# A fused attention and expert kernel: the last two batches get a program of their own

## The chip, the cores and the metric

One NeuronCore of a Trainium2 chip. The metric is the device time of the kernel in microseconds (us); a comparison takes the median of several runs.

## The reference

32 batches of 256 tokens with 128 features. Attention with 16 heads of 8 features, with a cubic "stablemax" in place of softmax, then four experts of which each token uses the best two by a router:

```python
x = x + attn_ref(layernorm(x), w_qkv, w_out, b_out)
x = x + ffn_ref(layernorm(x), router_w, router_b, w1, w3, w2)
# ffn_ref, for T tokens, E = 4 experts, F = 512, K = 2:
probs = softmax(xf @ router_w + router_b)
top_p, top_i = top_k(probs, K);  top_p = top_p / sum(top_p)
gates = zeros((T, E)).at[arange(T)[:, None], top_i].add(top_p)
h = silu(einsum('td,edf->etf', xf, w1)) * einsum('td,edf->etf', xf, w3)
expert_out = einsum('etf,efd->etd', h, w2)
out = einsum('te,etd->td', gates, expert_out)
```

All is float32.

## The kernel before

Every engine has a program written out by hand (blocks `sync`, `gpsimd`, `scalar`, `vector`, `tensor`), and the engines meet at semaphores. Each program is a chain of slots n = -2 to 33, a `first_half` and a `second_half` each; `over_batches` unrolls the first six and the last six and loops over those between. A slot works on several batches at once: in slot n the scores and weights of batch n are in hand, batch n-1 has its attention output, residual sum, second normalization and router, and batch n-2 has its experts. So slots 32 and 33 hold little but the experts: in slot 32 those of batch 30 and the attention output of batch 31, in slot 33 the experts of batch 31 alone.

TensorE. `weighted_values(i, off, g)` (L926) multiplies group g of the weights with the values, g = 0, 1, 2 in the second half of slot n and g = 3 early in the next slot. The output is transposed (L1022), normalized by VectorE, transposed again (L1033), multiplied by the output projection (L1043). The residual sum is normalized and transposed (L1105), and the router product is L1121. The up projections of a batch are eight units u = 0 to 7, each an a half (`up_a_unit`, w1) and a b half (`up_b_unit`, w3) of six matmuls (L908; each operand is split in a high and a low part and three of the four products are taken). Unit 0 runs at the end of a slot's second half, units 1 to 7 in the next first half. All a halves go to one bank `up_a`; b halves to `up_b`, with units 3, 5 and 7 in a third bank. The down projection `down(c, e)` (L1090) sums the four experts in one accumulation per block c of 128 tokens, in `up_b`; so the gate has to be in the hidden values before it. A matmul of float32 operands shows as two records.

ScalarE. SiLU of an a half (L554), the copies of the attention output (L581, L594), the logarithm and exp of the four groups of weights (L608, L613, the weights are exp(-log(...))), and ln and exp of the small inverse square roots (L623, L626) and of the router (L640). SiLU and exp/log need different tables, loaded at L538 and L604.

VectorE. `hidden(u)` (L677) multiplies the SiLU with the b half into `hid`; `normalized` (L696, L701), `attention_added` (L713), `statistics` (L752, L755), the router's steps ending in `gates` (L837 to L847), and `experts_added` (L786), which adds the down projection of both blocks to `y_acc`.

GpSimd. `gate_hidden` (L422) multiplies a unit of `hid`, where tokens run along the free axis, with `gate_all`, the gates copied to all partitions. It also does the inverse square root's Newton steps (L460 to L479), the scaling by it (L484), the split of the normalized sum (L497, L500) and the ranks of the router (L505 to L517).

SyncE issues the DMAs, among them the gates to `gate_scratch` in memory (L394), `gate_all` from it (L342) and the store of `y_acc` (L389).

Of the kernel before, what the change touches and what calls it, by code (L numbers as in the profile page):

```python
# [5 lines left out]
def attention_then_experts_kernel(nc: bass.Bass, x: bass.AP, w_qkv: bass.AP, w_out: bass.AP, b_out: bass.AP,  # L6
# [32 lines left out]
    C = S // 128  # L39
    G = H // 4  # L40
    FB = F // 128
    NB = E * FB
    U = G * C
# [6 lines left out]
    UP = NB // 2  # L50
# [8 lines left out]
    with ctx:  # L59
# [24 lines left out]
        q_tile = sb("q_tile", [128, G, S], F32R)  # L84
# [54 lines left out]
        spare = banks[:, 1:3, :].rearrange("p a t -> p (a t)")  # L139
        router_out = up_b[:, C * D:C * D + C * E].rearrange("p (c e) -> p c e", c=C)  # L140
        misc = ctx.enter_context(nc.psum_tensor("misc", [128, 512], F32))
        b_bank = [banks[:, 2, :] if u in (3, 5, 7) else up_b for u in range(UP)]
        score_buf = [(sc[:, 0, :], sc[:, 1, :], spare)[u % 3] for u in range(U)]

# [75 lines left out]
        gated = sem("gated")  # L220
        down_full = sem("down_full")
        acc_ok = sem("acc_ok")
        stored = [sem(f"stored{i}") for i in range(2)]

        TILED = 16 * 2 * TERMS
# [8 lines left out]
        def has(i, off):  # L234
            return not isinstance(i, int) or 0 <= no(i, off) < B
# [10 lines left out]
        def over_batches(eng, half_a, half_b):  # L246

            for n in range(-2, 4):  # L250
                half_a(n // 2, n % 2)
                half_b(n // 2, n % 2)
            with eng.Fori(2, B // 2 - 2) as i:
                for off in range(2):
                    half_a(i, off)
                    half_b(i, off)
            for n in range(B - 4, B + 2):
                half_a(n // 2, n % 2)
                half_b(n // 2, n % 2)


        def blank_stacks(eng, par):
# [27 lines left out]
        def _(sp):  # L290
# [82 lines left out]
            def second_half(i, off):  # L373
                n = no(i, off)
                m_split_at = value(n + 2)
                added, out_at = value(n - 1), address((n - 2) * S * D)
                gates_at, gates_read = value(GATE * n), value(16 * (n - 1))
                xn_used, x_from = value(n + 3), address((n + 3) * S * D)
                if has(i, off + 3):
                    sp.wait_ge(xn_ok, xn_used)  # L380
                    sp.dma_start(x_in[:], batch_at(x, x_from)).then_inc(x_loaded, 16)
                if has(i, off + 1):
                    par = (off + 1) % 2
                    sp.wait_ge(m_ok, m_split_at)
# [5 lines left out]
                if has(i, off - 1):  # L390
# [3 lines left out]
                    sp.dma_start(gate_scratch, gates[par][:].rearrange("p c e -> p (c e)")).then_inc(gates_out, 16)  # L394

            over_batches(sp, first_half, second_half)
            for par in range(2):
                sp.wait_ge(stored[par], 16 * (B // 2))

# [2 lines left out]
        def _(pool):  # L402
# [49 lines left out]
            def second_half(i, off):  # L452
# [69 lines left out]
                if has(i, off):  # L522
# [4 lines left out]
                        last = nc.gpsimd.tensor_tensor(x_resb[:, c, :], x_res[:, c, :], b_out_all[:], ALU.add)  # L527
                    last.then_inc(xres_ok, 1)

            over_batches(pool, first_half, second_half)  # L530


        @block.scalar
        def _(act):
# [66 lines left out]
            def second_half(i, off):  # L601
# [31 lines left out]
                for g in range(G):  # L633
# [7 lines left out]
                    if has(i, off):  # L641
                        weights_of(g)

            act.wait_ge(consts_v, 1)
            over_batches(act, first_half, second_half)


        @block.vector
        def _(dve):
# [81 lines left out]
            def second_half(i, off):  # L731
# [156 lines left out]
                if has(i, off + 3):  # L888
                    input_statistics(n + 3)

            dve.wait_ge(consts_ok, 4)
            over_batches(dve, first_half, second_half)


        @block.tensor
        def _(pe):
# [35 lines left out]
            def up(u, dst, hi, lo, full):  # L932

                for half in range(2):
                    e, f = divmod(2 * u + half, FB)
                    fs = slice(f * 128, (f + 1) * 128)
                    last = exact(dst[:, half * S:(half + 1) * S], (hi[:, e, fs], lo[:, e, fs]),
                                 (xn2_hi[:], xn2_lo[:]))
                last.then_inc(full, 1)

            def up_a_unit(i, off, u):
# [6 lines left out]
            def up_b_unit(i, off, u):  # L948
                m = no(i, off)
                if u < 3:  # L950
                    after(pe, hid_ok, UP * m + u)
                elif u == 3:
                    pe.wait_ge(o_ok, min(m + 2, B) if isinstance(i, int) else m + 2)
                else:
                    pe.wait_ge(hid_ok, UP * m + u - 1)
                if u == 0:
                    after(pe, acc_ok, m)
                    pe.wait_ge(lg_ok, m + 1)
                up(u, b_bank[u], w3_hi, w3_lo, b_full)

            def distances(i, off, u):

# [89 lines left out]
            def second_half(i, off):  # L1052
# [80 lines left out]
                def queries_and_keys():  # L1133
                    m = n + 2
                    pe.wait_ge(xnT_ok, m + 1)
                    if has(i, off + 1):
                        pe.wait_ge(m_ok, n + 2)
                    nc.tensor.matmul(misc[:, 0:S], proj_T[:, 0, :], xn_T[:], start=True, stop=True)
                    nc.tensor.matmul(misc[:, S:2 * S], proj_T[:, 1, :], xn_T[:], start=True,
                                     stop=True).then_inc(qk_full, 1)  # L1140
# [30 lines left out]
                    up_b_unit(i, off - 1, 0)  # L1171
                if has(i, off + 2):
                    queries_and_keys()
                if has(i, off) and not (isinstance(i, int) and n == 0):
                    weighted_values(i, off, 2)

            over_batches(pe, first_half, second_half)


# [25 lines left out]
```

## Time and profile before

| | |
|---|---|
| median of three runs | 1187.17 us (1183.64 to 1187.72) |
| the profiled execution | 1186.13 us, span 1184.4 us |
| TensorE busy | 1108.0 us (94%), 10116 matmul records |
| VectorE busy | 970.1 us (82%) |
| ScalarE busy | 1007.1 us (85%) |
| GpSimd busy | 736.9 us (62%) |
| costliest group | L422 on GpSimd, 256 times, 405.4 us, 1624 ns each |

The span runs from the first to the last instruction of one profiled execution. Busy times of TensorE are modelled at the end of each record, and records overlap. A chain row is a piece of the work that ended last, followed backwards from the last instruction. "PE" is TensorE, "DVE" VectorE, "ACT" ScalarE, "POOL" GpSimd, "SPq" the DMA issues of SyncE.

### The profile page before, as it was taken

The page shows a single profiled execution, that of the slowest core. Times are in us where ns is not written, and L with a number is a line of the kernel's source. Part 1 is how long each engine was busy: PE and PEld are TensorE (multiplying, and loading weights), DVE is VectorE, ACT ScalarE, POOL GpSimd, SP SyncE. Part 2 cuts the span into 40 slices and gives each one's busy share as a digit, 9 for nine tenths or more (in the row PEclk, how much of TensorE's full clock was granted, in tenths as well). Part 3 has the DMA queues.
Part 4 walks back from the last instruction along what each step waited for, and adds up shares of the span by engine and source line. Part 5 has one row for each costly group of instructions (what it writes and reads, how often), then busy time and mean ns, then how long its engine had stood idle before and what let it go on. Part 6 is the DMA issues. An engine that isn't in the chain of part 4 may idle for free.

```text
span 1184.4 us, 29551 instructions
## 1 busy us (share of the span) xinstructions
PE 1108.0 (94%) x10116; PEld 945.0 (80%) x10116; DVE 970.1 (82%) x1804; ACT 1007.1 (85%) x1033; POOL 736.9 (62%) x961
## 2 busy tenths in 40 slices
PE   2468999999999999999999999999999999999987
PEld 1346888888888888888888888888888888888876
DVE  4577898988888898888889888889898888989632
ACT  0578999888999998899999888999988889998852
POOL 5415576766656767665676766667676666666564
PEclk9997999999999999999999999999999999999999
DMA  4523223333322333333223333322333332233000
GB/s 122 195 82 105 90 86 111 118 116 116 104 89 89 95 115 116 121 105 92 90 85 115 119 118 110 97 90 80 116 116 116 115 101 89 89 98 112 29 24 28
DMA packets 129779, 118.57 MB, mean 100 GB/s; under 512 B 15880, under 2 KB 124104, under 8 KB 129736
## 3 DMA queue, kind: packets, MB, share of 16 engines
q1 hardware_dynamic: 128584, 116.97, 31.8%
q10 hardware_dynamic: 1152, 1.05, 0.3%
q8 instruction: 25, 0.41, 0.1%
q14 instruction: 18, 0.15, 0.0%
HBM read 95.75 MB, written 21.10 MB: 99 GB/s over the span
## 4 chain that ended last, share of the span: by engine, by line
POOL 32%; PE 27%; issue 20%; DMA 11%; DVE 4%; SPq 2%; ACT 2%; POOLq 1%; DVEq 0%; ACTq 0%
POOL hid L422 20%; PE banks L1090 11%; DMA gate_all<-gate_scratch 10%; PE banks L908 5%; PE banks L926 3%; POOL qk_split L441 3%; PE sc L975 3%; PE sc L1075 2%; POOL qk_split L438 2%; POOL xn_lo L500 1%; DVE mx L761 1%; POOL xn_hi L497 1%; POOL x_resb L527 1%; PE misc L1105 1%; ACT w_sq L546 1%
## 5 line engine op out<-in xcount | busy, mean ns | idle before, releaser
L422 POOL TENSOR_TENSOR hid<-hid,gate_all 128x512 f32<-128x512 f32 x256 | 405.4, 1624 | 190.9 <-DMA gate_all<-gate_scratch 168.4
L685 DVE SCALAR_TENSOR_TENSOR poly<-w_sq,sc 128x1024 f32<-128x1024 f32 x256 | 308.5, 1216 | 54.0 <-ACT w_sq L546 50.2
L546 ACT ACTIVATE w_sq<-sc 128x1024 f32<-128x1024 f32 x256 | 259.5, 1027 | 103.5 <-PE sc L975 98.4
L908 PE MATMUL banks<-xn_hi,w_hi 128*128 128x256 f32 x1024 | 303.7, 297 | 9.8 <-issue 6.3
L908 PE MATMUL banks<-xn_hi,w_lo 128*128 128x256 f32 x1024 | 288.7, 282 | 0.0
L908 PE MATMUL banks<-xn_lo,w_hi 128*128 128x256 f32 x1024 | 288.3, 282 | 0.0
L1090 PE MATMUL banks<-w_sb,hid 128*128 128x128 f32 x2048 | 258.5, 280 | 9.6 <-POOL hid L422 8.2
L1090 PEld LDWEIGHTS banks<-w_sb,hid 128*128 128x128 f32 x2048 | 238.1, 192 | 26.6 <-POOL hid L422 14.7
L608 ACT ACTIVATE poly<-poly,two 128x2048 f32<-128x2048 f32 x128 | 254.9, 1991 | 0.4
L613 ACT ACTIVATE poly<-poly 128x2048 f32<-128x2048 f32 x128 | 242.6, 1896 | 0.0
L761 DVE TENSOR_REDUCE mx<-sc 128x4 f32<-128x1024 f32 x192 | 227.3, 1214 | 14.5 <-PE sc L1075 8.7
L908 PEld LDWEIGHTS banks<-xn_hi,w_hi 128*128 128x128 f32 x1024 | 193.5, 189 | 36.2 <-issue 25.0
L908 PEld LDWEIGHTS banks<-xn_lo,w_hi 128*128 128x128 f32 x1024 | 193.6, 189 | 0.0
L908 PEld LDWEIGHTS banks<-xn_hi,w_lo 128*128 128x128 f32 x1024 | 192.5, 188 | 0.0
L677 DVE TENSOR_TENSOR hid<-silu_a,banks 128x512 f32<-128x512 f32 x256 | 171.7, 680 | 18.3 <-PE banks L908 13.6
L975 PE MATMUL sc<-q_stack,k_pad 128*128 128x256 f32 x1024 | 171.6, 296 | 10.8 <-DVE poly L685 5.5
L554 ACT ACTIVATE silu_a<-banks 128x512 f32<-128x512 f32 x256 | 153.3, 599 | 15.3 <-PE banks L908 12.0
L975 PEld LDWEIGHTS sc<-q_stack,k_pad 128*128 128x128 f32 x1024 | 140.5, 194 | 26.6 <-issue 13.9
L926 PE MATMUL banks<-poly,v_pad 128*32 128x256 f32 x2048 | 140.1, 393 | 1.6 <-ACT poly L613 1.6
L926 PEld LDWEIGHTS banks<-poly,v_pad 128*32 128x32 f32 x2048 | 54.4, 110 | 44.4 <-ACT poly L613 11.2
L1075 PE MATMUL sc<-k_tile,q_tile 32*128 32x256 f32 x768 | 67.8, 341 | 23.4 <-DVE mx L761 8.7
L761 DVE TENSOR_REDUCE mx<-banks 128x4 f32<-128x1024 f32 x64 | 77.8, 1216 | 0.0
(96 smaller groups left out, 1127.5 us busy)
## 6 DMA issues: line engine op xcount, KB each, us to landing
qk_scratch<-qk_split SPq DMA_DIRECT2D x32, 512.0 KB, 3.1
k_tile<-qk_scratch SPq DMA_DIRECT2D x128, 128.0 KB, 2.5
k_pad<-qk_scratch SPq DMA_DIRECT2D x256, 64.0 KB
gate_all<-gate_scratch SPq DMA_DIRECT2D x32, 512.0 KB, 4.4
q_tile<-qk_scratch SPq DMA_DIRECT2D x124, 128.0 KB, 2.5
q_stack<-qk_scratch SPq DMA_DIRECT2D x124, 128.0 KB
x_in<-in_L_attn_x_dram SPq DMA_DIRECT2D x32, 128.0 KB, 2.1
x_res<-in_L_attn_x_dram SPq DMA_DIRECT2D x32, 128.0 KB, 2.2
```

The lines of the kernel that those rows point to most:

```text
L422: nc.gpsimd.tensor_tensor(h, h, by_token.unsqueeze(1).to_broadcast([128, 2, C, 128]), ALU.mult).then_inc(gated, 1)
L546: nc.scalar.activation(w_sq[:, u % 2, :], sc[:, u % 2, :], ACT.Square).then_inc(sq_ok, 1)
L554: nc.scalar.activation(silu_a[:, u % 2, :], up_a[:], ACT.Silu).then_inc(silu_ok, 1)
L608: nc.scalar.activation(poly[:, C * g:C * (g + 1), :], poly[:, C * g:C * (g + 1), :], ACT.Ln, bias=two[:]).then_inc(ln_ok, 1)
L613: nc.scalar.activation(poly[:, C * g:C * (g + 1), :], poly[:, C * g:C * (g + 1), :], ACT.Exp, scale=-1.0).then_inc(p_ok, 1)
L677: nc.vector.tensor_tensor(hid[:, 2 * u:2 * u + 2, :].rearrange("p a t -> p (a t)"), silu_a[:, u % 2, :], b_bank[u], ALU.mult).then_inc(hid ...
L685: nc.vector.scalar_tensor_tensor(poly[:, u, :], w_sq[:, u % 2, :], 3.0, sc[:, u % 2, :], ALU.add, ALU.mult).then_inc(poly_ok, 1)
L761: nc.vector.tensor_reduce(by_row[:, :, :, u], score_buf[u].rearrange("p (j c t) -> p j c t", j=2, c=C), AX.X, ALU.min, negate=True).then_i ...
L908: last = nc.tensor.matmul(dst, lhs[a], rhs[b], start=(k == 0), stop=(k == len(terms) - 1))
L926: last = nc.tensor.matmul(pv[32 * j:32 * j + 32, g // 2, :], v_pad[par][:, c, 4 * g + j, first:first + 32], poly[:, 2 * g + j // 2, at:at ...
L975: last = nc.tensor.matmul(sc[:, u % 2, at:at + S], k_pad[par][:, u, j, c * 128:(c + 1) * 128], q_stack[par][:, u, :], start=True, stop=True)
L1090: last = nc.tensor.matmul(up_b[:, c * D:(c + 1) * D], hid[:, FB * e + f, c * 128:(c + 1) * 128], w2_sb[:, FB * e + f, :], start=(e == 0 an ...
```

## The change

`over_batches` now ends after slot 31, and each engine gets a `drain()` in place of slots 32 and 33. Batches 30 (`LATE`) and 31 are done differently there:

- The hidden values aren't multiplied by gates. The down projection is made per expert (both blocks of an expert, an accumulation each, at a place of its own: experts 0 to 2 in the banks of `sc[:, 1]`, expert 3 in `banks[:, 2]`), and VectorE adds it times the gate, a scalar per token, to `y_acc`: `expert_added`, two operations per expert. `gate_hidden`, the write of the gates to memory and `gate_all` fall away for both batches.
- Up projections take turns over three pairs of banks (`late_sets`; the two of `sc` are free once the scores of batch 31 are used up): units 0 to 7 of batch 30 on pairs 0, 1, 2, 0, 1, 0, 1, 0, those of batch 31 on pairs 1, 0, 1, 0 and so on. Unit 1 of batch 30 is issued in slot 31, ahead of the third weighted values.
- The attention output of batch 31 is laced between units of batch 30 in a new order on TensorE, ScalarE and VectorE. VectorE also does the scaling of the normalized sum and its split in high and low part (which GpSimd did), with the split parts of batch 31 in `q_tile`.
- The gates of batch 31 are made last on VectorE, after its last hidden values; its exp (with a table load) follows its last SiLU on ScalarE.

The core of the diff (the SyncE drain is the two stores; the GpSimd drain holds the same small Newton and rank steps as before, without scaling and split):

```diff
-            for n in range(B - 4, B + 2):
+            for n in range(B - 4, B):
                 half_a(n // 2, n % 2)
                 half_b(n // 2, n % 2)
+        LATE = B - 2
+        def late_set(m, u):
+            if m == LATE:
+                return late_sets[(0, 1, 2, 0, 1, 0, 1, 0)[u]]
+            return late_sets[1 - u % 2]
+        def late_used(m, u):
+            v = UP * (m - LATE) + u
+            return UP * LATE + (v - 1 if v >= 5 else v - 2)
...
+            def drain():
+                def silu(m, u):
+                    k = UP * m + u
+                    act.wait_ge(a_full, k + 1)
+                    after(act, hid_ok, k - 1 if u > 1 else k - u)
+                    nc.scalar.activation(silu_a[:, u % 2, :], late_set(m, u)[0], ACT.Silu).then_inc(silu_ok, 1)
+                act.preload_act_table_set("silu_and_others")
+                act.wait_ge(pv_full, G * B)
+                act.wait_ge(oq_full, B - 1)
+                nc.scalar.copy(o_T[:], pv).then_inc(o_ok, 1)
+                silu(LATE, 0)
+                silu(LATE, 1)
+                act.wait_ge(attnT_full, B)
...
+                nc.scalar.copy(attn_T[:], misc[:, 0:S]).then_inc(attnT_ok, 1)
+                silu(LATE, 2)
+                silu(LATE, 3)
+                act.preload_act_table_set("natural_log_exp_and_others")
+                act.wait_ge(var_ok, k + 1)
+                nc.scalar.activation(ln_var[:, s], var_eps[:, s], ACT.Ln).then_inc(lnv_ok, 1)
...
+                nc.scalar.activation(rstd0[:, s], ln_var[:, s], ACT.Exp, scale=-0.5).then_inc(rstd0_ok, 1)
+                act.preload_act_table_set("silu_and_others")
+                for u in range(4, UP):
+                    silu(LATE, u)
+                for u in range(UP):
+                    silu(m, u)
+                act.preload_act_table_set("natural_log_exp_and_others")
+                act.wait_ge(shift_ok, m + 1)
...
+                nc.scalar.activation(exp_l[:], shifted[:], ACT.Exp).then_inc(exp_ok, 1)
...
+                def expert_added(b, e):
+                    at = (C * E - 1) * (b - LATE) + C * e
...
+                    dve.wait_ge(late_down, E * (b - LATE) + max(e + 1, E - 1))
+                    for c in range(C):
+                        if e > 0:
+                            dve.wait_ge(summed, at - C + c + 1)
+                        op = nc.vector.scalar_tensor_tensor(y_acc[b % 2][:, c, :], late_expert(c, e),
+                                                            gates[b % 2][:, c, e:e + 1], y_acc[b % 2][:, c, :],
+                                                            ALU.mult, ALU.add)
+                        op.then_inc(acc_ok if (c, e) == (C - 1, E - 1) else summed, 1)
+
+                normalized()
+                hidden(LATE, 0)
+                hidden(LATE, 1)
+                hidden(LATE, 2)
+                attention_added()
+                statistics()
+                hidden(LATE, 3)
+                normalized_sum()
+                hidden(LATE, 4)
+                up_operand()
+                hidden(LATE, 5)
+                router()
+                hidden(LATE, 6)
+                hidden(LATE, 7)
+                hidden(m, 0)
+                for e in range(E - 1):
+                    expert_added(LATE, e)
+                hidden(m, 1)
+                expert_added(LATE, E - 1)
+                for u in range(2, UP):
+                    hidden(m, u)
+                chosen_gates()
+                for e in range(E):
+                    expert_added(m, e)
...
+            def late_up_a(m, u):
+                if m == LATE and u < 3:
+                    pe.wait_ge(poly_ok, U * B)
+                else:
+                    pe.wait_ge(silu_ok, late_used(m, u))
...
+            def late_up_b(m, u):
+                if m > LATE or u > 2:
+                    pe.wait_ge(hid_ok, late_used(m, u))
...
+                if isinstance(i, int) and n == B - 1:
+                    late_up_a(LATE, 1)
+                    late_up_b(LATE, 1)
                 if has(i, off) and not (isinstance(i, int) and n == 0):
                     weighted_values(i, off, 2)
...
+            def drain():
...
+                weighted_values(m // 2, m % 2, 3)
+                late_up_a(LATE, 2)
+                pe.wait_ge(o_ok, B)
...
+                last.then_inc(oq_full, 1)
+                late_up_b(LATE, 2)
+                late_up_a(LATE, 3)
+                pe.wait_ge(attn_ok, B)
...
+                last.then_inc(attnT_full, 1)
+                late_up_b(LATE, 3)
+                pe.wait_ge(attnT_ok, B)
...
+                last.then_inc(res_full, 1)
+                ups(LATE, 4)
+                down(LATE, 0)
+                ups(LATE, 5)
+                pe.wait_ge(xn2_ok, B)
...
+                last.then_inc(xn2T_full, 1)
+                ups(LATE, 6)
+                pe.wait_ge(xn2_out, B)
...
+                last.then_inc(lg_full, 1)
+                down(LATE, 1)
+                ups(LATE, 7)
+                down(LATE, 2)
+                ups(m, 0)
+                ups(m, 1)
+                down(LATE, 3)
+                for e in range(E - 1):
+                    ups(m, 2 * e + 2)
+                    ups(m, 2 * e + 3)
+                    down(m, e)
+                down(m, E - 1)
```

## Rows read from the trace of the kernel before

**Rows 1.** The page: TensorE's busy time, and the chain's shares by engine
```profile
PE 1108.0 (94%) x10116; PEld 945.0 (80%) x10116; DVE 970.1 (82%) x1804; ACT 1007.1 (85%) x1033; POOL 736.9 (62%) x961
...
POOL 32%; PE 27%; issue 20%; DMA 11%; DVE 4%; SPq 2%; ACT 2%; POOLq 1%; DVEq 0%; ACTq 0%
```

**Rows 2.** The chain in order of time, end of the run: start us, us, what
```profile
1108.43 1.44 PE banks L908 x12
...
1131.38 0.18 DVE gates L847
1131.58 2.52 DMA gate_scratch<-gates
1134.12 3.84 DMA gate_all<-gate_scratch
1138.03 9.37 POOL hid L422 x6
...
1150.90 3.84 PE banks L1090 x32
...
1164.57 9.32 POOL hid L422 x6
...
1176.90 4.75 PE banks L1090 x40
1181.67 0.42 DVE y_acc L786
```

**Rows 3.** Busy time of each engine by stages of the end; the first line names columns
```profile
core 0: us, PE busy (x) PEld busy (x) DVE busy (x) ACT busy (x) POOL busy (x), PEclk, DMA share, GB/s
...
1117.00:1132.54 15.54, 13.13 (x131) 10.78 (x131) 3.75 (x20) 15.48 (x13) 8.91 (x19) 1.00 0.04 10
1132.54:1150.90 18.36, 16.67 (x135) 14.74 (x135) 7.39 (x17) 8.57 (x14) 12.76 (x11) 1.00 0.10 30
...
1157.06:1171.86 14.80, 13.28 (x96) 11.87 (x96) 5.80 (x16) 6.81 (x11) 8.35 (x10) 1.00 0.14 46
1171.86:1182.09 10.23, 7.92 (x66) 7.37 (x64) 1.27 (x3) 0.66 (x1) 4.99 (x4) 1.00 0.00 0
1132.54:1182.09 49.55, 43.16 (x340) 39.21 (x340) 15.65 (x40) 16.12 (x25) 29.68 (x31) 1.00 0.08 25
```

**Rows 4.** TensorE in order of time, three places
```profile
1128.20 0.39 PE L908 MATMUL banks<-xn_hi,w_hi 128*128 128x256 f32 x1
1128.42 0.28 PE L908 MATMUL banks<-xn_lo,w_hi 128*128 128x256 f32 x1
...
1132.54 1.07 PE L926 MATMUL banks<-poly,v_pad 128*32 128x256 f32 x16 [0.82 <-ACT poly L613]
...
1154.57 0.38 PE L1105 MATMUL misc<-ident,xn 128*128 128x128 f32 x2
```

**Rows 5.** ScalarE in order of time: start us, us, line, operation, [idle before it]
```profile
1130.59 1.89 ACT L613 ACTIVATE poly<-poly 128x2048 f32<-128x2048 f32 x1
1132.50 1.28 ACT L538 ACT_TABLE_LOAD   x1
1133.80 0.60 ACT L554 ACTIVATE silu_a<-banks 128x512 f32<-128x512 f32 x1
1134.29 0.58 ACT L581 COPY o_T<-banks 128x512 f32<-128x512 f32 x1
...
1165.62 0.60 ACT L554 ACTIVATE silu_a<-banks 128x512 f32<-128x512 f32 x1 [1.07 <-PE banks L908]
```

**Rows 6.** VectorE and GpSimd in order of time: hidden product, addition, statistics, Newton's last step
```profile
1143.32 0.69 DVE L677 TENSOR_TENSOR hid<-silu_a,banks 128x512 f32<-128x512 f32 x1 [1.08 <-PE banks L908]
1144.71 0.49 DVE L713 TENSOR_TENSOR y_acc<-misc,x_resb 128x128 f32<-128x128 f32 x2 [0.71 <-PE misc L1043]
...
1148.54 0.25 DVE L755 BATCH_NORM_AGGREGATE mean_var<-stats 128x2 f32<-128x6 f32 x2
...
1151.62 0.19 POOL L479 TENSOR_TENSOR rstd<-rstd,newton 128x2 f32<-128x2 f32 x1
```

More of the change, by code:

```diff
@@ L389, in second_half @@
                     sp.dma_start(batch_at(out, out_at), y_acc[par][:]).then_inc(stored[par], 16)
-                if has(i, off - 1):
+                if has(i, off - 1) and not (isinstance(i, int) and n == B - 1):
                     par = (off - 1) % 2
@@ L394, in second_half @@
                     sp.dma_start(gate_scratch, gates[par][:].rearrange("p c e -> p (c e)")).then_inc(gates_out, 16)
+            def drain():
+                for m in (B - 2, B - 1):
+                    sp.wait_ge(acc_ok, m + 1)
+                    sp.dma_start(batch_at(out, m * S * D), y_acc[m % 2][:]).then_inc(stored[m % 2], 16)
             over_batches(sp, first_half, second_half)
+            drain()
             for par in range(2):
@@ L891, in _ @@
             dve.wait_ge(consts_ok, 4)
             over_batches(dve, first_half, second_half)
+            drain()
         @block.tensor
@@ L1173, in second_half, with drain, ups, down @@
                     queries_and_keys()
+                if isinstance(i, int) and n == B - 1:
+                    late_up_a(LATE, 1)
+                    late_up_b(LATE, 1)
                 if has(i, off) and not (isinstance(i, int) and n == 0):
                     weighted_values(i, off, 2)
+            def drain():
+                m = B - 1
+                def ups(b, u):
+                    late_up_a(b, u)
+                    late_up_b(b, u)
+                def down(b, e):
+                    pe.wait_ge(hid_ok, UP * b + FB // 2 * (e + 1) + (1 if b == LATE and e == 0 else 0))
+                    if b == LATE and e == E - 1:
+                        pe.wait_ge(lg_ok, B)
+                    if b > LATE and e == 0:
+                        pe.wait_ge(summed, C * (E - 1))
+                    if b > LATE and e == E - 1:
+                        pe.wait_ge(acc_ok, B - 1)
+                    for c in range(C):
+                        for f in range(FB):
+                            last = nc.tensor.matmul(late_expert(c, e), hid[:, FB * e + f, c * 128:(c + 1) * 128],
+                                                    w2_sb[:, FB * e + f, :], start=(f == 0), stop=(f == FB - 1))
+                    last.then_inc(late_down, 1)
+                weighted_values(m // 2, m % 2, 3)
+                late_up_a(LATE, 2)
+                pe.wait_ge(o_ok, B)
+                pe.wait_ge(xn2_out, m)
+                for c in range(C):
+                    for a in range(G // 2):
+                        at = (c * G // 2 + a) * 128
+                        last = nc.tensor.transpose(misc[:, at:at + 128], o_T[:, a, c * 128:(c + 1) * 128], ident[:])
+                last.then_inc(oq_full, 1)
+                late_up_b(LATE, 2)
+                late_up_a(LATE, 3)
+                pe.wait_ge(attn_ok, B)
+                for c in range(C):
+                    last = nc.tensor.transpose(misc[:, c * 128:(c + 1) * 128], attn[:, c, :], ident[:])
+                last.then_inc(attnT_full, 1)
+                late_up_b(LATE, 3)
+                pe.wait_ge(attnT_ok, B)
+                for c in range(C):
+                    last = nc.tensor.matmul(misc[:, c * D:(c + 1) * D], attn_T[:, c * 128:(c + 1) * 128],
+                                            proj_T[:, 3, :], start=True, stop=True)
+                last.then_inc(res_full, 1)
[3 more added lines that the diff above has]
+                pe.wait_ge(xn2_ok, B)
+                pe.wait_ge(y_ok, C * B)
+                for c in range(C):
+                    last = nc.tensor.transpose(misc[:, c * 128:(c + 1) * 128], xn2[:, c, :], ident[:])
+                last.then_inc(xn2T_full, 1)
+                ups(LATE, 6)
+                pe.wait_ge(xn2_out, B)
+                for c in range(C):
+                    last = nc.tensor.matmul(late_router[:, c, :], xn2_T[:, c * 128:(c + 1) * 128], rw[:],
+                                            start=True, stop=True)
+                last.then_inc(lg_full, 1)
[10 more added lines that the diff above has]
+                down(m, E - 1)
```

144 lines of the change are left out of this document (141 added, 3 removed).

## The prediction

> **What bounds the kernel now.** I read the page first. TensorE is busy 94% of the span, but the chain that ended last puts only 27% on it and 32% on GpSimd [rows 1]. A chain share is read with its place, so next comes the chain in order of time over the end of the run, since the change touches nothing before the second half of slot 31. From 1131.38 on, the chain leaves TensorE twice and takes the same way both times: gates ready, written to memory (2.52), read back by all partitions (3.84), then gate multiplications on GpSimd (six of them 9.37, so 1.56 each), and only then the down projections: 32 records starting at 1150.90 for batch 30, 40 records starting at 1176.90 for batch 31. Then comes one addition by VectorE of 0.42 and the store [rows 2]. In the middle of a run such a trip is beside other work; here nothing is left to put beside it. Third, the stages: from 1132.54 (last weighted values) to 1182.09 (last addition done) are 49.55 us, in which GpSimd is busy 29.68, ScalarE 16.12 and VectorE 15.65 [rows 3]. TensorE shows 43.16, but its records overlap and their ends are modelled, so I don't take that as its need. I count its slots: 12 records of an up-projection unit take 1.44 [rows 2], 32 down records from 1150.90 to the next TensorE record at 1154.57 take 3.67, so 0.115 each [rows 2, 4]. The expert work of a batch is thus 8 units (11.5) and 64 down records (7.3). Also, in the stretch of batch 31's units ScalarE's SiLUs come 1.67 apart (0.60 and 1.07 idle waiting for TensorE) where a unit needs 1.44 [rows 2, 5]: there is one bank for the a half, so SiLU and next unit take turns.
>
> **What the change removes.** Of batches 30 and 31: 16 gate multiplications (about 25 us of GpSimd by the 1.56 each), two gate writes, two broadcasts. The end of the run no longer waits for any of them. What is late next is TensorE itself, if every hand-over is covered, so I add up its slots from the point that the change can't move. That point is 1132.54: the last weighted values start there because the last exp (1.89 from 1130.59) ends at 1132.48 [rows 4, 5], and ScalarE's chain ahead of it is untouched.
>
> **Unit 1 of batch 30 is moved** ahead of that point. TensorE is done with unit 0 at about 1129.7 (start 1128.20 [rows 4], 1.44 and a restart of 0.1) and would otherwise wait; the unit takes until 1131.2, the third weighted values (1.0) until 1132.2, still before 1132.48. Priced at nothing. The stretch 1117.00 to 1132.54 has 15.54 us and 13.13 of TensorE in it [rows 3]. Without that cover it would cost 1.44.
>
> **TensorE from 1132.54 on.** Last weighted values 1.0. 14 units (2 to 7 of batch 30, 8 of batch 31) of 1.44: 20.2. 8 experts of down projection, 16 records of 0.115: 14.7. Attention output of batch 31 (4 transposes, 2 transposes, 2 products, 2 transposes of the normalized sum, router), about 14 records with the two-record steps at 0.22 [rows 4]: 1.6. Sum 37.5. The first record of a unit after another kind of matmul or a wait takes 0.22 to the next one in place of 0.12 (1128.20 to 1128.42 [rows 4]). The new order changes kind about ten times: 1.0. Sum 38.5.
>
> **Hand-overs that are not covered.** (a) The output copy on ScalarE: a table load ends at 1133.78, the copy now goes first and takes 0.58, so 1134.4 [rows 5]. TensorE has 1.0 and half a unit until 1134.35: stall 0.1. (b) Normalization on VectorE, a reciprocal and two multiplications (about 0.8, two operations of this size take 0.49 [rows 6]), is covered by a unit's worth of work, but the first hidden product (0.69 [rows 6]) is queued behind it and half b of unit 3 waits for that product: 0.2 to 0.3. (c) From the output product to the normalized sum: hidden 2 ahead in the queue 0.3, addition 0.49, statistics about 0.8 ending with the 0.25 of [rows 6], two GpSimd steps 0.5, ln and exp on ScalarE 0.4, four GpSimd steps at 0.27 apart that end as the one at 1151.62 does [rows 6], two scalings about 0.5, and six hand-overs of 0.05 to 0.1: about 4.6. TensorE's cover is unit 4, expert 0's down, unit 5: 1.5 + 1.8 + 1.5 = 4.8. Covered by 0.2, priced at nothing, at 1 us each us if it is late. (d) ScalarE needs two table loads of 1.28 around that ln and exp. The first lies before the variance is there. The second puts SiLU 4 at about 1142.4, and unit 6 needs it at about 1143.2. (e) Router: 0.1. Sum of stalls 0.5. TensorE's last down record starts to end at 1132.54 + 38.5 + 0.5 = 1171.5, result there at 1171.7.
>
> **The Trainium skill on (d).** The row shows a SiLU 1.30 after the start of a load [rows 5], so load and nothing more. The Trainium skill, page "ScalarE: Activation LUTs", section "What ACT_TABLE_LOAD costs", adds a drain of about 1.38 us, 2.66 per switch. By it, an estimate, unit 6 would stall 0.6 and the last gates would be 1.4 later, together about 2 us on the total. The trace disagrees with it and the sum goes by the trace.
>
> **VectorE's own end.** After SiLU 7 of batch 31 (half a of unit 7 ends at about 1167.2, SiLU done 1168.0) ScalarE loads the exp table (1.28) and makes the exp (0.2): 1169.4. Four gate steps of about 0.2 (0.18 and a hand-over [rows 2]): 1170.3. Three experts' additions, six operations 128x128 with a gate as scalar. The trace has no such operation: from below the 0.18 of the smallest, from above 0.35 with a wait in front of each; nearest is the addition of 128x128 from PSUM, 0.49 for two, so 0.245 [rows 6], which I take. 1.5: 1171.8. So VectorE is ready when TensorE is, 1171.7, and two more additions give 1172.3, with 0.35 each 1173.1. Elsewhere VectorE has room: it gains some 3 us of additions and 1.3 us of splitting and scaling on 15.65 of 49.55.
>
> **The sum.** Last addition done 1172.3 against 1182.09 [rows 2], store and end unchanged (2.3): span 1174.6, 9.8 less. Against the profiled execution's 1186.1 that is 1176.3; against the median of the runs shown, 1187.2, it is 1177.4. I forecast 1176.9, between the two since the profiled run lies inside the spread of the runs: 0.9% faster.
>
> **Rivals.** (1) The hand-overs of (c) and (d) are exposed. For it: the margin in (c) is 0.2 us and each engine takes its queue in order, so a late SiLU delays the ln, and a late product delays the statistics. Against: what is queued there is short. 3 us more: 1180. (2) VectorE and the exp bound the end, with 0.35 per addition and later gates, 1 to 2 us more: 1178.5. (3) The change does not do what it says: the three pairs of banks don't separate the units and they go on at 1.67. 14 times 0.23 is 3.2; with 3 us of exposed hand-overs the gain is 3.6: 1183, which can't be told from no change. Against it: the waits written are for the unit two back, whose product is done about 0.8 after that unit's end, while the next unit takes 1.44. (4) The other side, slower: the clock of TensorE falls. Its place is the hand-overs of batch 31's attention between short bursts; at the lower of its two levels (1.2 in place of 2.4 GHz) the 38 us of matmuls would double: about +28, 1215. It decides from 16 us of matmuls at the lower level on (the gain of 9.8 and 5.9 more). Against it: the granted clock is 1.00 in every stretch, also from 1171.86 to 1182.09, where TensorE is busy only 7.92 of 10.23 with one long stop [rows 3], and the new stops are shorter. The Trainium skill, page "TensorE: Matmul & The Clock Gate", section "A second HAM failure mode: psum-queue depth-cycling", says that cycling through PSUM banks with short idles between groups can make the clock oscillate; by it rival 4 would come true here. The trace doesn't agree: units with SiLU turns between them ran at 1.00 from 1157.06 to 1171.86 [rows 3].
>
> **Numbers.** Forecast 0.72, rival 1 0.12, rival 2 0.05, rival 3 0.08, rival 4 0.03. A measurement of this kernel can tell about 0.5% (5.9 us) from no change. Faster by over 0.5% are the forecast and rivals 1 and 2, 0.89, less 0.03 for a baseline whose runs spread over 4 us: 0.86. Within 0.5% rival 3 and that part: 0.11. Slower 0.03. Range: no restarts and no stalls (1.5 less) and a run at the fast side of the spread (2 less) give 1173.4; rival 1 with a slow run gives 1181.5.
>
> **What would show it.** In the changed profile: no gate_all after batch 29; the chain over the last 40 us nearly all TensorE, with its idle time there under 1 us; SiLUs of batch 31 about 1.5 apart, with longer pauses only at the down projections; last weighted values still at 1132.5; last down record near 1171.5, two additions and the store behind it. Wrong would be: stops of TensorE before the transposes of the normalized sum or before unit 6 (rival 1), a gap between the last down record and the last additions (rival 2), a granted clock under 1.00 (rival 4), or a later last exp (my fixed point).

## The result, and the profile after

The changed kernel took 1172.22 us (median of 4 runs, 1171.58 to 1176.53) against 1185.41 for the kernel before (4 runs, 1183.56 to 1187.72): ratio 0.9894, 95% interval [0.9875, 0.9913]. Its profiled execution took 1176.53, with a span of 1174.5. So the profile is where the sum put it (span 1174.6, 1176.3), and the median lies 4.7 us under the forecast of 1176.9 and 1.2 under the range. Most of what follows asks how both can be. Over all runs of this study, these included, 16 of the changed kernel have a median of 1174.6, and 73 of the kernel before one of 1186.7.

The page of the changed kernel (span; busy time; chain by engine):

```profile
span 1174.5 us, 29545 instructions
...
PE 1104.5 (94%) x10116; PEld 944.1 (80%) x10116; DVE 975.1 (83%) x1822; ACT 1006.6 (86%) x1033; POOL 709.2 (60%) x941
...
POOL 29%; PE 28%; issue 21%; DMA 10%; DVE 4%; ACT 4%; SPq 2%; POOLq 1%; ACTq 0%; DVEq 0%
```

As in [rows 1], the shares of the whole run say next to nothing: 32% on GpSimd has become 29%. The stage from the last weighted values to the last addition, which was 49.55 long with 43.16 of TensorE and 29.68 of GpSimd [rows 3], says all (columns as there):

```profile
1133.47:1172.20 38.73, 37.79 (x328) 36.62 (x328) 20.10 (x58) 15.71 (x25) 2.23 (x11) 1.00 0.02 5
1133.47:1145.83 12.36, 12.36 (x109) 11.39 (x110) 7.52 (x20) 8.84 (x14) 1.17 (x6) 1.00 0.00 1
1145.83:1166.27 20.44, 20.44 (x178) 20.44 (x179) 8.38 (x24) 4.79 (x8) 1.06 (x5) 1.00 0.03 8
1166.27:1172.20 5.93, 4.99 (x44) 4.79 (x43) 4.20 (x14) 2.09 (x3) 0.00 (x0) 1.00 0.00 0
```

10.8 us are gone, TensorE is never idle up to 1166.27 but for some 0.15 that its overlapping records hide, and the granted clock is 1.00 in all of it. The chain of the changed kernel, with the two trips of [rows 2] gone:

```profile
1133.47 1.07 PE banks L1157 x16
1134.54 0.90 PE sc L1139 x6
1135.44 0.58 PE misc L1456 x4
...
1142.23 1.44 PE banks L1139 x12
1143.67 0.22 PE misc L1476 x2
...
1156.99 1.43 PE banks L1139 x12
1158.42 1.78 PE sc L1445 x16
...
1168.92 0.22 ACT exp_l L736
...
1169.84 0.18 DVE gates L1079
...
1171.60 0.34 DVE y_acc L1091
```

It is TensorE's from 1133.47 to 1166.27, then it passes to ScalarE and VectorE: the last exp, the gates, the additions.

The stage starts 0.93 later than the 1132.54 from which the sum was made. The new program didn't move it. ScalarE's first square of slot 2 (the square of the scores, 1.03 us, eight in a slot) stands 0.93 later too, in the kernel before and in the changed one:

```profile
105.67 1.94 ACT L546 ACTIVATE w_sq<-sc 128x1024 f32<-128x1024 f32 x2 [1.89 <-PE sc L975]
106.60 1.94 ACT L605 ACTIVATE w_sq<-sc 128x1024 f32<-128x1024 f32 x2 [2.19 <-PE sc L1223]
```

A stage that is 1.0 shorter than forecast and a start that is 0.9 later cancel; that the span met the forecast to 0.1 is luck.

### The profile page after: what moved, and what is told of

It is laid out like the page before. It is cut to its first block, busy times and chain, and to the rows that moved or that the text cites. A ratio compares the mean times of both kernels' runs of the same rounds, so it can differ in the third digit from the quotient of the medians.

```text
span 1174.5 us, 29545 instructions
## 1 busy us (share of the span) xinstructions
PE 1104.5 (94%) x10116; PEld 944.1 (80%) x10116; DVE 975.1 (83%) x1822; ACT 1006.6 (86%) x1033; POOL 709.2 (60%) x941
## 4 chain that ended last, share of the span: by engine, by line
POOL 29%; PE 28%; issue 21%; DMA 10%; DVE 4%; ACT 4%; SPq 2%; POOLq 1%; ACTq 0%; DVEq 0%
POOL hid L449 18%; PE banks L1338 10%; DMA gate_all<-gate_scratch 9%; PE banks L1139 5%; POOL qk_split L468 3%; PE banks L1157 3%; PE sc L1223 2%; PE sc L1323 2%; POOL qk_split L465 2%; POOL xn_lo L527 1%; ACT poly L667 1%; DVE mx L856 1%; POOL xn_hi L524 1%; POOL x_resb L554 1%; DVE poly L780 1%
## 5 line engine op out<-in xcount | busy, mean ns | idle before, releaser
L449 POOL TENSOR_TENSOR hid<-hid,gate_all 128x512 f32<-128x512 f32 x240 | 380.5, 1620 | 178.3 <-DMA gate_all<-gate_scratch 148.3
L1139 PE MATMUL banks<-xn_hi,w_hi 128*128 128x256 f32 x976 | 288.8, 296 | 6.4 <-issue 6.4
L1139 PE MATMUL banks<-xn_hi,w_lo 128*128 128x256 f32 x976 | 275.4, 282 | 0.0
L1139 PE MATMUL banks<-xn_lo,w_hi 128*128 128x256 f32 x976 | 274.8, 282 | 0.0
L1338 PE MATMUL banks<-w_sb,hid 128*128 128x128 f32 x1920 | 242.9, 280 | 7.0 <-POOL hid L449 5.7
L1338 PEld LDWEIGHTS banks<-w_sb,hid 128*128 128x128 f32 x1920 | 223.4, 192 | 23.2 <-POOL hid L449 11.9
L1139 PEld LDWEIGHTS banks<-xn_lo,w_hi 128*128 128x128 f32 x976 | 184.6, 189 | 0.0
L1139 PEld LDWEIGHTS banks<-xn_hi,w_lo 128*128 128x128 f32 x976 | 183.5, 188 | 0.0
L772 DVE TENSOR_TENSOR hid<-silu_a,banks 128x512 f32<-128x512 f32 x240 | 161.0, 681 | 1.8 <-ACT silu_a L613 1.1
L613 ACT ACTIVATE silu_a<-banks 128x512 f32<-128x512 f32 x240 | 143.7, 599 | 0.7
```

Source lines behind the costliest of these rows:

```text
L449: nc.gpsimd.tensor_tensor(h, h, by_token.unsqueeze(1).to_broadcast([128, 2, C, 128]), ALU.mult).then_inc(gated, 1)
L613: nc.scalar.activation(silu_a[:, u % 2, :], up_a[:], ACT.Silu).then_inc(silu_ok, 1)
L772: nc.vector.tensor_tensor(hid[:, 2 * u:2 * u + 2, :].rearrange("p a t -> p (a t)"), silu_a[:, u % 2, :], b_bank[u], ALU.mult).then_inc(hid ...
L1338: last = nc.tensor.matmul(up_b[:, c * D:(c + 1) * D], hid[:, FB * e + f, c * 128:(c + 1) * 128], w2_sb[:, FB * e + f, :], start=(e == 0 an ...
```

## Experiments

Stage below is the time from the start of the last weighted values to the end of the last addition in each profile: 49.55 before, 38.73 after.

**The same kernels again.**

> The kernel before, unchanged. Its eight times so far fall in two groups, near 1183.6 and near 1187.5, 4 us apart. Theory A (start of the run): the groups come from where TensorE's clock is at its lower level in the first 105 us. In the profiled execution it was low for 17 us there. Then a profiled execution whose span is near 1181 has a shorter low stretch, and every row after the first 110 us is shifted by the same amount. Rival B (spread over the whole run): DMA or queue jitter in the loop; then the shift grows along the run and the clock rows of the start are the same. Ratio to the kernel before: 1.000 by either, within 0.2%.

> The changed kernel, unchanged. Its profiled execution spanned 1174.5 (predicted 1174.6), but three of four times were near 1171.9. Theory A: it has the same two groups as the kernel before, and the four runs drew the short one three times; the ratio of like with like is 1176.5/1187.5 or 1171.9/1183.6, both 0.990, a gain of 11 to 12 us. Rival C: the gain is 9.8 us as my sum has it and the rest of the 13 us is the draw; then the ratio over many runs settles near 0.9917. Measured from the last weighted values of batch 31 to the end of the last addition, the stage was 49.55 us before and 38.73 us after (10.8 less); a new profile should repeat 38.7 within 0.2 whichever group it is in.

The kernel before: 1187.07 (12 runs), ratio to itself 1.001 [0.9996, 1.0024]; 23 other executions of it on the same chip have a median of 1184.67, so a median can move by 2.4 with no change at all. The changed kernel: 1174.6 (6 runs), ratio 0.9913 [0.9898, 0.9929]. The stage of the changed kernel repeated to 0.01 us (last weighted values 1131.31, last addition done 1170.03, so 38.72). That of the kernel before didn't: its last weighted values start 0.7 earlier than in [rows 4], at 1131.84, and its last addition ends 0.9 later, so its stage is 51.2. Its first square of slot 2 is 0.9 earlier than in the first profile and the first of slot 31 0.7, so the shift doesn't grow along the run, as rival B would have it. Rival C (a gain of 9.8) falls with the stages: 10.8 less, and 12.5 less between the two repeats. A row of TensorE and one of VectorE in order of time in that repeat:

```profile
1176.21 6.36 PE L1090 MATMUL banks<-w_sb,hid 128*128 128x128 f32 x40 [1.79 <-POOL hid L422]
1182.61 0.42 DVE L786 TENSOR_TENSOR y_acc<-banks,y_acc 128x256 f32<-128x256 f32 x1 [10.52 <-PE banks L1090]
```

and stretches of it (columns as in [rows 3]; the granted clock is the third number from the end):

```profile
1173.00:1175.50 2.50, 1.42 (x13) 1.23 (x11) 0.00 (x0) 0.00 (x0) 2.50 (x3) 1.00 0.00 0
1175.50:1177.00 1.50, 0.79 (x5) 0.79 (x6) 0.00 (x0) 0.00 (x0) 0.65 (x1) 0.90 0.00 0
1177.00:1179.00 2.00, 2.00 (x12) 2.00 (x11) 0.00 (x0) 0.00 (x0) 0.00 (x0) 0.50 0.00 0
1179.00:1181.00 2.00, 2.00 (x15) 2.00 (x15) 0.00 (x0) 0.00 (x0) 0.00 (x0) 0.72 0.00 0
```

The 40 records that took 4.75 in [rows 2] take 6.36: behind the stop for the gate multiplications the clock was granted at 0.50 for 3.4 us. In the execution that I had read, the first profile, it happened not to. Neither theory A nor rival B had this; what A says of the start comes below. I call the new one theory D: this stop makes the clock fall in some executions, and the change removed the stop and with it the fall.

**The stop filled.**

> The kernel before with 7 needless transposes of the identity (14 records, about 1.6 us at the upper clock level) in TensorE's last stop, between its third and fourth step of the last down projection, into a bank that is free. Theory D (the clock falls in that stop in some executions): in the repeat of the kernel before, the last 40 records took 6.38 us at a granted clock of 0.50, in its first profile 4.75 at 1.00. With the stop filled they take 4.75 always, the slower executions come down by up to 1.6 us, and the median falls by about 0.5 to 1 against the kernel before (0.9993 or so); the stop itself stays, since GpSimd is what ends it. Rival E (the fall comes from the many shorter stops between batch 31's units before it): the clock still falls in some executions, and the median doesn't move.

```diff
+                    if isinstance(i, int) and n == B + 1 and c == 0 and e == E - 1:
+                        for _ in range(7):
+                            nc.tensor.matmul(sc[:, 0, 0:128], ident[:], ident[:], start=True, stop=True)
                     if c == 0:
                         pe.wait_ge(gated, UP * m + FB // 2 * (e + 1))
```

1185.97 (12 runs), 0.9994 [0.9983, 1.0006] of the kernel before: the ratio alone says nothing. The mean granted clock of each execution does: of 69 executions of the kernel before for which it was noted, 38 have 0.981, 0.990 or 0.991, of these 12 none: 10 have 0.993, and 2 have 0.982, which the long lower stretch at the start explains by itself (in the profiled one from 46.9 to 70.8, beside the usual one up to 101.5). Not every 0.991 is a fall at the end, though: the changed kernel has it in 3 of 16, and in its profile with 0.991 the clock was low for 20.5 us at the start and never after 103.6. The values 0.981 and 0.990 (17 of the 69) occur in none of the 16. So the fall came in at least 17 and at most 38 of the 69. The highest time is 1186.6, where the kernel before beside it reached 1188.7. The profile has the stop filled and the 40 records in 4.73:

```profile
1176.69 4.73 PE L1093 MATMUL banks<-w_sb,hid 128*128 128x128 f32 x40 [0.23 <-POOL hid L422]
```

So D holds, and rival E falls: the shorter stops before it, unchanged here, didn't bring it. In the kernel before the fall costs 1.6 us where it happens, so 0.4 to 0.9 in the mean.

**Without the trip of the gates.**

> The kernel before without the gates of batches 30 and 31: their hidden values go into the down projection as they are, with no gate multiplication on GpSimd, no gate write and no broadcast; slots, banks and order stay. The output of the last two batches therefore lacks the gates. Theory 1 (order and banks carry most): TensorE still has units 1.67 apart, the end of slot 32 still waits for the normalized sum, and only the idle time before the down projections goes, about 0.7 in slot 32 and 2.0 + 0.8 in slot 33, with 1 to 1.5 for the split of the normalized sum that starts sooner: the stage from the last weighted values to the last addition falls from 49.55 to about 45, and the time by 4 to 5 us (0.996). Rival 2 (the trip is the whole gain): the stage falls to 40 and the time by 9 to 10 us (0.992).

```diff
-                    if c == 0:
+                    if c == 0 and isinstance(i, int) and n >= B:
+                        pe.wait_ge(hid_ok, UP * m + FB // 2 * (e + 1))
+                    elif c == 0:
                         pe.wait_ge(gated, UP * m + FB // 2 * (e + 1))
```

(and no gate multiplication, gate write or broadcast for the two batches, so the kernel leaves their gates out). 1181.62 (10 runs), 0.997 [0.9957, 0.9983]; stage 46.63, from 1132.12 to 1178.75. Theory 1 in its direction, and less than it gave: 2.9 of the stage's 10.8, where I had expected 4 to 5. The chain shows why: slot 33 isn't held by the down projection's end but by VectorE's queue, in which hidden product 0 stands behind the gate steps of the router.

```profile
1157.51 0.25 POOLq L59
...
1157.79 0.18 DVE chosen L837
...
1158.49 0.70 DVE hid L677
...
1159.24 0.99 PE banks L908 x6
```

Taken out of the old order, the trip that leads the chain of [rows 2] was worth less than a third of what the new program brought. The other 7.9 are what the drain does beside that: order, banks, and the scaling and split on VectorE. The next two runs price unit 1 and the banks; the rest wasn't taken apart, nor was the trip priced inside the new order, where it could cost more.

**Unit 1 issued late, and one pair of banks.**

> The changed kernel with unit 1 of batch 30 issued behind the last weighted values and not in slot 31. Theory 1 (TensorE's slots bound the new end): the stage from the last weighted values to the last addition grows by a unit less what stalls it fills, from 38.7 to about 40.0. Rival 2 (the chain over ScalarE and VectorE bounds it): the stage stays at 38.7 to 39.0. Time within 0.2% of the changed kernel either way.

```diff
-                if isinstance(i, int) and n == B - 1:
-                    late_up_a(LATE, 1)
-                    late_up_b(LATE, 1)
...
                 weighted_values(m // 2, m % 2, 3)
+                late_up_a(LATE, 1)
+                late_up_b(LATE, 1)
                 late_up_a(LATE, 2)
```

Stage from 1131.23 to 1171.28, 40.05, so 1.32 longer, as theory 1 had it (40.0); 1175.77 (4 runs). TensorE's slots are what this stage is made of: a unit more costs nearly the whole unit.

> The changed kernel with units 4 to 7 of batch 30 and all of batch 31 on one pair of banks, so each a half waits for the SiLU before it and each b half for the hidden product before it. Theory 1 (the banks carry a part of the gain): each of six unit pairs without a down projection between them loses 0.3 to 0.5, and the stage grows from 38.7 to about 41, the time by 2 to 2.5 us against the changed kernel. Rival I (the down projections between the pairs give all the slack that is needed): under 0.5.

```diff
-            if m == LATE:
-                return late_sets[(0, 1, 2, 0, 1, 0, 1, 0)[u]]
-            return late_sets[1 - u % 2]
+            if m == LATE and u < 4:
+                return late_sets[(0, 1, 2, 0)[u]]
+            return late_sets[0]
...
-            return UP * LATE + (v - 1 if v >= 5 else v - 2)
+            return UP * LATE + (v if v >= 4 else v - 2)
```

Stage from 1129.69 to 1173.14, 43.45: 4.7 longer, twice what I expected; 1178.25 (4 runs) against 1174.6. The chain:

```profile
1137.10 0.70 DVE hid L996
...
1137.84 0.98 PE banks L1139 x6
1138.82 1.79 PE sc L1445 x16
...
1143.52 0.60 DVE hid L996
...
1144.16 0.98 PE banks L1139 x6
...
1150.60 3.19 PE banks L1139 x24
```

Four pairs of units take 3.19 in place of 2.85 (1.43 and 1.42), 1.4 in all, which is what I had thought of. The other 3.3 are lost earlier: with one pair, half b of units 4 and 6 has to wait for a hidden product that stands in VectorE's queue behind the statistics or the split. Here the second and third pair brought most where VectorE's queue was long.

**Gates early.**

> The changed kernel with the exp and the gates of batch 31 made before its first unit (ScalarE has idle time of 2.6 us there, which holds the two table loads), so that only additions are left at the end. Theory 1 (VectorE and ScalarE bound the very end, by 0.3): the last additions wait for TensorE alone; the stage from the last weighted values to the last addition falls from 38.7 to about 38.4. Rival G (TensorE bound it, and the gates were hidden): no change, 38.7. Rival H (the two more table loads delay SiLU 0 of batch 31 and the units behind it): 39.2 or more. The time can't tell these apart, the profile can.

```diff
+                act.preload_act_table_set("natural_log_exp_and_others")
+                act.wait_ge(shift_ok, m + 1)
...
+                act.preload_act_table_set("silu_and_others")
                 for u in range(UP):
                     silu(m, u)
...
                 hidden(LATE, 7)
+                chosen_gates()
                 hidden(m, 0)
```

From the start of the last exp of the weights to the end of the span: 42.65 (1129.89 to 1172.54) against 42.96 and 42.95 in the profiles of the changed kernel, so 0.3 less, theory 1. 1174.11 (4 runs).

**The start kept warm.**

> The changed kernel with needless transposes of the identity laid into TensorE's waits of slots 0 and 1 (the first 100 us), into a bank that isn't used yet. Theory A (the rest of the spread is the clock of the start): in every profile so far TensorE stands at the lower level from about 80 or 90 to 100 us, with its own work on the chain for the last 7 us of it. Kept at the upper level it saves about 3 us: time near 1170.5 to 1171.5 where the changed kernel has 1172 to 1176, with executions within 1 us of each other, and the 16th square of ScalarE (start of slot 2) at 102 where it was at 104.3 to 106.6. Rival F (GpSimd, DMA or load jitter of the start sets the offset): the spread of 3 to 4 us stays and the time with it.

```diff
+            def warm(i, off, count):
+                if isinstance(i, int) and 0 <= no(i, off) < 2:
+                    for _ in range(count):
+                        nc.tensor.matmul(banks[:, 0, 0:128], ident[:], ident[:], start=True, stop=True)
...
+                    if u > 2:
+                        warm(i, off, 2)
...
+                    warm(i, off, 5 if g == 0 else 3)
```

1171.76 (5 runs, 1169.91 to 1173.22), 0.9882 [0.9863, 0.9902]. In its profile slot 2 starts 4 to 6 us earlier than in the three of the changed kernel. All profiles side by side, by the time at which the clock rises for good, and the 17th of ScalarE's 1.03 us squares (first of slot 2):

| profile | upper level from | square |
|---|---|---|
| kernel before | 102.5 | 105.7 |
| its repeat | 101.5 | 104.8 |
| stop filled, no gate trip | 101.5, 102.1 | 105.0, 105.1 |
| changed kernel | 103.6 | 106.6 |
| its repeats | 100.8, 102.1 | 104.2, 105.3 |
| unit 1 late, gates early | 101.0, 101.5 | 104.3, 104.9 |
| one pair of banks | 96.7 | 102.6 |
| warm start | 67.4 | 100.4 |
| kernel before with warm start (below) | 100.0 | 103.4 |
| all together (below) | 98.1 | 101.6 |

The square follows the rise by 3.0 to 3.5 us in all but one pair (5.9) and this warm start. From that square on, slots are 34.3 us apart in all of them (33.9 for the first one of the warm start), and the square of slot 31 is as far apart between two profiles as that of slot 2, to 0.6 us. So the start is where the profiles of one kernel differ (theory A for this part), and rival F falls: with more of the start at the upper level, the time falls. Whether the spread shrinks is hardly shown: 3.3 us in five executions here, 3.6 and 3.9 in the two sets of six of the changed kernel. Nor do the needless matmuls keep the clock up each time. The profiled execution is the fastest of the five; three of them have a mean clock below 0.997, and in the two later profiles with the same matmuls the clock was low from 89.7 to 100.0 and from 91.2 to 98.1.

**Both together, and the start alone on the kernel before.**

> The changed kernel once more, on the chip of the two that follow, so that they have it beside them. Ten times so far lie from 1171.6 to 1176.5 with a median of 1174.1. Theory A+D (both kernels have the variable start, only the kernel before has the falling clock at the end): 1171.6 to 1176.5 again, against a kernel before of 1183 to 1188.5, ratio 0.990 to 0.991.

> The kernel before with the same needless transposes in TensorE's waits of slots 0 and 1 as the changed kernel had. Theory A+D: the start gives 2 to 3 us here too, the end still takes its slower form in some executions: 1180.5 to 1186, median about 1183.5 against 1186. The 16th square at about 100.4. Rival J (the gain of those transposes is the changed kernel's alone): no difference.

> The changed kernel with three additions: the needless transposes in slots 0 and 1, the gates of batch 31 made early, and the last expert's second block in a bank of its own (of the first pair, free by then), so that VectorE adds and SyncE stores the first block while TensorE still works on the second. By the terms measured so far: start 2 to 3 us less, gates 0.3, last block 0.3: stage from the last weighted values to the last addition 38.1, time near 1171 (median of the changed kernel 1174.1). Rival K (the smaller last store takes as long as the whole one): the same to 0.1, since only the addition is shortened.

On one chip: the changed kernel 1175.26 (6 runs, 1172.17 to 1176.09), 0.9901 [0.9878, 0.9924]; the kernel before with the warm start 1184.22 (12 runs), 0.998 [0.9966, 0.9995], and its profile had the fall at the end again; all together 1171.21 (5 runs, 1170.23 to 1172.53), 0.9873 [0.9849, 0.9898], with 42.51 from the last exp of the weights to the end. The chain row of the last 40 down records with the warm start, at the lower level again:

```profile
1175.17 6.37 PE banks L1097 x40
```

So rival J falls: the transposes brought the kernel before 2.9 us. All together has the lowest median of this study, 4.05 us under the changed kernel beside it; 0.45 of that are the gates and the last block, the rest is the start. Against the warm start alone (1171.76, on another chip) it isn't clear of noise. Its stage is 38.30, where I had expected 38.1. The store of half the size landed in 1.6 in place of 1.8, but from the last addition to the end of the span it is 2.26 in place of 2.28, so rival K holds.

```diff
+            if b > LATE and (c, e) == (C - 1, E - 1):
+                return banks[:, 0, 0:D]
...
+                sp.wait_ge(summed, 2 * (C * E - 1))
+                sp.dma_start(block_at(m, 0), y_acc[m % 2][:, 0, :]).then_inc(stored[m % 2], 16)
```

## Why the prediction was right in its sum and wrong in its number

**The sum of the new end.** Predicted 39.8 (1132.54 to 1172.3), measured 38.73. The term that was mis-sized is the down projection: I took 3.67 for 32 records from a stretch that starts behind a stop, so 1.84 for an expert's 16, and by the starts below they take 1.70. Five of the eight experts do, two take 1.78 and 1.79: some 0.9 less in all. With stalls of 0.15 in place of 0.5, TensorE was done 1.4 sooner than summed (37.79 behind the start in place of 39.2); VectorE's end behind it took 0.94 in place of 0.6. TensorE in order of time in the changed kernel:

```profile
1140.29 1.95 PE L1445 MATMUL sc<-w_sb,hid 128*128 128x128 f32 x16
1141.99 0.37 PE L1139 MATMUL banks<-xn_hi,w_hi 128*128 128x256 f32 x1
1142.19 0.28 PE L1139 MATMUL banks<-xn_lo,w_hi 128*128 128x256 f32 x1
```

The restart is there (0.20 to the second record, where I had 0.22).

**The hand-overs.** (c) was covered, and by more than I gave it: the scalings ended at 1143.08, 0.4 before TensorE came to their transposes. (d) went as worked out, SiLU 4 begins 1.29 after its table load did. ScalarE and VectorE:

```profile
1141.15 0.20 ACT L727 ACTIVATE rstd<-ln_var 128x2 f32<-128x2 f32 x1
1141.37 1.28 ACT L728 ACT_TABLE_LOAD   x1
1142.66 0.60 ACT L708 ACTIVATE silu_a<-sc 128x512 f32<-128x512 f32 x1
```

```profile
1142.48 0.60 DVE L1036 TENSOR_SCALAR xn<-y_acc,mean_var,rstd 128x128 f32<-128x128 f32 x2 [0.92 <-POOL rstd L570]
...
1170.04 1.64 DVE L1091 SCALAR_TENSOR_TENSOR y_acc<-sc,gates,y_acc 128x128 f32<-128x128 f32 x6
1171.60 0.60 DVE L1091 SCALAR_TENSOR_TENSOR y_acc<-banks,gates,y_acc 128x128 f32<-128x128 f32 x2
```

The drain of 1.38 that the Trainium skill's page "ScalarE: Activation LUTs" adds to a load (section "What ACT_TABLE_LOAD costs") doesn't appear here: the load starts 0.02 behind the end of the activation before it, and the SiLU 1.29 behind the load's start.

**The very end.** An addition with a gate costs 0.26 (1170.04 to 1171.60 for six), where I took 0.245. TensorE's last result is there at 1171.26 and VectorE begins its last two at 1171.60, so VectorE binds by 0.3: a small rival 2, as the gates made early confirm.

**Unit 1** was free, and late it costs 1.32 (I had 1.44). **Rival 1** and **rival 3** didn't happen: no stop before the transposes of the normalized sum. **Rival 4** didn't happen in the changed kernel: in none of the eight profiles that have its new end did that end run under 1.00. **The fixed point** held against the change, not against the start: the last weighted values follow the first square of slot 31 by 31.95 to 31.97 in every profile of this study, but counted from the start of the run they begin at 1133.47, 1131.31 and 1132.33 in the three profiles of the changed kernel.

**What failed** is the step from the sum to the time, at the lower end of the range: 2 us for "a run at the fast side of the spread". The 16 executions of the changed kernel spread over 4.9 us, 1171.58 to 1176.53, and its three profiled ones, with spans of 1174.5, 1173.3 and 1172.3, differ as their first squares of slot 2 do (106.6, 105.3, 104.2): the start makes the difference between them, and I had 2 us for it. Three of the first four executions (1171.58, 1171.89 and 1172.56) are among the five fastest of the 16, so the first median was a lucky draw, 2.4 us under the 1174.6 of all 16, which lies inside the range. The profiled execution was the slowest of the four, which is why the sum seemed to agree with it.

Under the draw stand two errors of mechanism or size. The stage fell by 10.8 and not by 9.8, and most of that 1.0 is the down records. And I wrote that "the granted clock is 1.00 in every stretch, also from 1171.86 to 1182.09", which was true of that execution alone: in 17 to 38 of 69 others the stop at the end brought the clock down, 0.4 to 0.9 us in the mean that the change also removes. I had the clock as a risk of the new kernel and not as a cost of the old one. Of the 4.7 us between forecast and median, 2.4 are the draw, 1.0 the stage, 0.4 to 0.9 the fall of the clock; the remaining 0.4 to 0.9 I can't assign.

## What to carry to other kernels

Count an engine's slots by starts inside a full stream, and compare the stage that changes between profiles, not the whole time: that of the changed kernel repeated to 0.02 us in three profiles (38.72 to 38.74) where times spread over 5. Repeat the kernel before too: its stage was 49.55 once and 51.2 once. A chain that names a trip names what is late, not what its removal brings: without it, the stage fell by 2.9 of 10.8. A median of four executions is not one of sixteen; a range for it has to hold the whole spread. Before a stop of TensorE is priced by its length, look at more than one execution for what the clock does behind it.

## What the hardware showed that I had not expected

A stop of 1.79 us by the profile, at the end of 4.8 us in which TensorE worked only 24 records, was followed in some executions by 3.4 us at the lower level, and with 1.6 us of needless matmuls in it none of 12 executions showed the mean clock of such a fall. The Trainium skill's page "TensorE: Matmul & The Clock Gate", section "HAM oscillation — how this bites in real kernels", describes DMA waits of 3 to 5 us between bursts of matmuls after which the next burst runs cold. The trace agrees in what follows, with 6.36 against 4.73 for the same 40 records, but the stop here was shorter, and it didn't come each time. And in the first 105 us, the time at which the clock rises for good moved between 96.7 and 103.6 from one profile to the next; the first square of slot 2 moved with it, from 102.6 to 106.6, and the rest of a kernel of 1186 us keeps these 4 us. Why the phase differs between executions, no run here shows.
